# Two tables of x from the host, a scale from squares, and GpSimd for one third of the low halves

## What is computed

```
h = x @ W + b_W;  xi, xj = split(h)
xji = (xj[src] + (edge_attr @ W_e + b_We)) / (in_degree[dst] + 1e-6)
x  = layernorm(x + xi + segment_sum(xji, dst))
h2 = x @ W1;  deg counts the edges and one self loop per node
out = segment_sum(h2[src] * rsqrt(deg)[src] * rsqrt(deg)[dst], dst) + b1
y  = leaky_relu(batchnorm(out) * gamma + beta, 0.01)
result = layernorm(x + y)
```

## Time and profile before

| what | value |
|---|---|
| median of 3 runs | 936.38 us (935.14 to 938.89) |
| the profiled execution | 936.68 us, of which the span of the trace is 934.6 us |
| busy share of the span | PE 95%, DVE 72%, ACT 48%, POOL 37% |
| DMA | 244.77 MB, mean 262 GB/s |

### The profile page before, as it was taken

How to read it: one execution, slowest core, us unless ns; L and a number is a source line. 1 busy time by engine, 2 the same in 40 slices (tenths; PEclk the granted TensorE clock), 3 DMA queues, 4 the chain that set the end, 5 groups by cost and what they waited for, 6 DMA issues and landing times.

```text
span 934.6 us, 30500 instructions
## 1 busy us (share of the span) xinstructions
PE 883.9 (95%) x12210; PEld 791.2 (85%) x12210; DVE 676.6 (72%) x1249; ACT 450.3 (48%) x983; POOL 349.4 (37%) x401
## 2 busy tenths in 40 slices
PE   4867999999999999999999999999999999999995
PEld 4756888888988898989899999999988888888874
DVE  6999899999999998899888899888842111112255
ACT  3764666656666665556565556565542000000026
POOL 2236444455554444455334455434332011112200
PEclk8988999999999999999999999999999999999998
DMA  6428999998879788777878758678667897779654
GB/s 180 110 83 296 361 345 320 317 342 290 313 247 319 284 311 283 229 229 241 253 264 277 223 185 301 214 274 282 209 216 299 343 358 279 272 260 326 249 155 136
DMA packets 96762, 244.77 MB, mean 262 GB/s; under 512 B 39560, under 2 KB 64838, under 8 KB 90726
## 3 DMA queue, kind: packets, MB, share of 16 engines
q1 hardware_dynamic: 95014, 239.46, 73.7%
q0 software_dynamic: 1600, 3.28, 1.4%
HBM read 183.85 MB, written 58.85 MB: 260 GB/s over the span
## 4 chain that ended last, share of the span: by engine, by line
PE 85%; DVE 5%; issue 3%; ACT 3%; DMA 1%; SPq 1%; ACTq 0%; DVEq 0%
PE x_ps L876 26%; PE pair_ps L951 19%; PE pair_ps L858 13%; PE e_ps L895 10%; PE x_ps L884 9%; PE j_ps L933 2%; PE j_ps L981 2%; DVE lo_oh L616 1%; DVE key_oh L619 1%; PE pair_ps L960 1%; PE j_ps L934 1%; ACT counts L1065 1%; PE u_vps L1409 1%; DMA counts_kept<-counts 1%; DMA streams<-in_x 1%
## 5 line engine op out<-in xcount | busy, mean ns | idle before, releaser
L1065 ACT CAST counts<-pair_ps 128x784 bf16<-128x784 f32 x391 | 315.3, 817 | 251.5 <-PE pair_ps L858 244.1
L876 PE MATMUL x_ps<-counts,xsplit 128*128 128x256 bf16 (+1 forms) x2450 | 307.5, 271 | 0.0
L616 DVE TENSOR_TENSOR lo_oh<-counter,lo_t 128x2048 bf16<-128x2048 bf16 x196 | 252.3, 1287 | 53.9 <-PE pair_ps L858 52.5
L876 PEld LDWEIGHTS x_ps<-counts,xsplit 128*128 128x128 f16 x2450 | 222.1, 98 | 29.3 <-issue 7.1
L858 PE MATMUL pair_ps<-key_oh,lo_oh 128*128 128x100 bf16 x3128 | 207.8, 209 | 22.5 <-ACT counts L1065 15.4
L858 PEld LDWEIGHTS pair_ps<-key_oh,lo_oh 128*128 128x128 bf16 x3128 | 182.8, 98 | 36.9 <-issue 15.0
L619 DVE TENSOR_TENSOR key_oh<-counter,key_t 128x1600 bf16<-128x1600 bf16 x196 | 196.4, 1002 | 0.0
L895 PE MATMUL e_ps<-streams 128*32 128x128 f32 x3528 | 106.9, 274 | 0.1
L884 PE MATMUL x_ps<-counts,zown 128*128 128x256 bf16 (+1 forms) x840 | 105.9, 269 | 0.1
L951 PE MATMUL pair_ps<-streams,zown 128*128 128x256 bf16 x878 | 99.0, 273 | 0.0
L895 PEld LDWEIGHTS e_ps<-streams 128*32 128x32 f32 x3528 | 93.3, 110 | 4.8 <-issue 1.0
(11 more groups left out here) (181 smaller groups left out, 890.6 us busy)
## 6 DMA issues: line engine op xcount, KB each, us to landing
streams<-in_edge_attr SPq DMA_DIRECT2D x196, 576.0 KB, 9.1
counts_kept<-counts SPq DMA_DIRECT2D x10, 1600.0 KB, 9.1
streams<-counts_kept SPq DMA_DIRECT2D x6, 1600.0 KB, 6.5
counts<-counts_kept SPq DMA_DIRECT2D x4, 1600.0 KB, 7.1
counts_kept<-counts SPq DMA_DIRECT2D x2, 3136.0 KB, 12.7
streams<-counts_kept SPq DMA_DIRECT2D x2, 3136.0 KB, 14.8
edst<-in_dst SPq DMA_DIRECT2D x196, 4.5 KB
streams<-in_x SPq DMA_DIRECT2D x3, 1024.0 KB, 5.7
```

Source lines behind the costliest of these rows:

```text
L616: dv.tensor_tensor(lo_oh[:, ring, :, :, :].rearrange("p r w k t -> p (r w) k t"), counter[:, :, :].unsqueeze(1).to_broadcast([P, g, P, 2]) ...
L876: last = nc.tensor.matmul(x_ps[:, 0, 0:n], xsplit[:, q // 2, q % 2, :], by_hi[:, q // 2, :], start=(q == 0), stop=(q == 2 * HS - 1))
L1065: a.copy(out.rearrange("p h (g n) -> p h g n", g=2), pair_ps[at % 2][:, :, 0:4 * KW].rearrange("p g (n h) -> p h g n", h=HI)[:, 0:HS]).the ...
```

## The change

The kernel gets x in two more forms, both laid out by the host with no arithmetic: `x_rows` (a node's features in one partition, as in `xrows`) and `x_columns` (features on partitions). The columns are loaded into the memory of `zown`, and `own_product` reads them there; `turn_x` and `x_turned` are gone. The scale comes from the sum of all squares, not from the largest magnitude: PE multiplies each tile's upper bf16 halves by themselves (`sum_squares`), DVE takes the diagonal (`add_squares`), PE sums over partitions, DVE makes the power of two on all partitions (`scales`). The largest magnitudes per row are taken for the check alone, from the high halves, in blocks 16, 18 and 20. The high halves are at slots 7, 9 and 11, two of the low ones on DVE at slots 14 and 16, the third on POOL in two passes. SP loads both tables before the edges, waits for the low halves by chunk, and issues `keep_counts(0)` before the last of those chunks; in later blocks `keep_counts` stands one place earlier, and the load of row starts later. `count_row` and `start_of` move from slots 9 and 10 to 11 and 12.

```diff
 X_PIECES = ((0, 8), (8, 16), (16, NB))
-LARGEST_AT = (None, 2, 4)
-TOP_AT, SCALES_AT, SPREAD_AT = 5, 8, 12
-HIGH_AT, LOW_AT = (11, 13, 15), (16, 18, 20)
+NORM_AT, TOTAL_AT, SCALES_AT = 7, 5, 8
+HIGH_AT, LOW_AT = (7, 9, 11), (14, 16)
+ROWS_CHECKED_AT = (16, 18, 20)
 OWN = [(h, min(4, HS - h)) for h in range(0, HS, 4)]
-OWN_FIRST = 4
+SQUARED_FIRST = 4
+OWN_IN = {**{s: s + 1 for s in range(9)}, **{SL + 1 + k: 10 + k for k in range(3)}}
+SQUARED_IN = {1: (4, 5, 6, 7), 3: (8, 9, 10, 11, 12)}
...
-        own = zown[:, :].bitcast(F32).rearrange("p (h f) -> p h f", f=F)
+        columns = zown[:, :].bitcast(F32)
+        own = columns.rearrange("p (h f) -> p h f", f=F)
...
-        turn_ps = [x_ps[:, :, :].rearrange("p a (b n) -> p (a b) n", n=P), e_ps]
+        own_ps = [j_ps, e_ps]
+        squares_ps, norm_ps = x_ps[:, 0, 0:P], x_ps[:, 1, 0:1]
+        upper_halves = zown[:, :].bitcast(BF16).rearrange("p (h n q) -> p h n q", n=P, q=2)[:, :, :, 1]
...
-            sp.dma_start(wi, W0[:, 0:F]).then_inc(S["wi_in"], 16)
-            load_inputs(sp, {"x": xf}, x, S, range(1))
+            load_pieces(sp, columns, x_columns, S["columns_in"], range(1))
             for b in range(2, ROW_RING):
                 load_rows(sp, b)
+            sp.dma_start(wi, W0[:, 0:F]).then_inc(S["wi_in"], 16)
             load_weights(sp, {"wj": wj, "we": we, "bi": bi, "bj": bje, "be": be_t[:, :]}, W0, b0, We, be, S)
             sp.wait_ge(win_in[0], 32)
-            load_inputs(sp, {"x": xf}, x, S, range(1, len(X_PIECES)))
+            load_pieces(sp, columns, x_columns, S["columns_in"], range(1, len(X_PIECES)))
+            load_pieces(sp, xf, x_rows, S["x_in"], range(len(X_PIECES)))
 
             def start_values(b):
                 sp.wait_ge(S["starts_known"], b + 1)
...
+            def load_edges(b, g, starts):
+                reach(sp, S["e_summed"], edge_group(b - 1, g) + 1)
+                for c in range(EG):
+                    if b == 0 and g == 1:
+                        sp.wait_ge(S["x_low"], [(c + 1) * EJ * F <= 2 * z * F for _, z in X_PIECES].index(True) + 1)
+                        if c == EG - 1:
+                            keep_counts(0)
+                    sp.dma_start(ebuf[g][:, c, :, :].rearrange("p j f -> p (j f)"),
+                                 ea[bass.ds(starts[g * EG + c], EE), :].rearrange("(p j) f -> p (j f)", j=EJ))\
+                      .then_inc(e_in[g], 16)
 
...
+            load_rows(sp, ROW_RING)
             for b in range(NB + 2):
                 u = b - 2
-                if b + ROW_RING < LATE:
-                    load_rows(sp, b + ROW_RING)
-                if b + ROW_RING == LATE:
-                    load_late_rows(sp)
                 if b < NB:
                     starts = start_values(b)
                     load_destinations(b, starts)
+                    if 2 <= b <= NB - 2:
+                        keep_counts(b - 1)
                     keep_inverse(b)
-                if 1 <= b <= NB - 2:
...
+                if b + ROW_RING + 1 < LATE:
+                    load_rows(sp, b + ROW_RING + 1)
+                if b + ROW_RING + 1 == LATE:
+                    load_late_rows(sp)
...
+            def split_low(k):
+                at = piece_tiles(k)
+                pool.wait_ge(S["x_high"], k + 1)
+                step(g.tensor_scalar(xrows[:, at, :], xrows[:, at, :], xscale[:, 0:1], None, ALU.mult))
+                pool.wait_ge(S["x_low"], k)
+                g.tensor_tensor(xsplit[:, at, 1, :], xrows[:, at, :], xsplit[:, at, 0, :], ALU.subtract)\
+                 .then_inc(S["x_low"], 1)
...
+                if b == 0:
+                    split_low(2)
...
+            def add_squares():
+                dve.wait_ge(S["squares_summed"], 1)
+                step(dv.tensor_tensor(x1_mem[:, 0, :], squares_ps, ident[:, :], ALU.mult))
+                dv.tensor_reduce(out=norm[:, :], in_=x1_mem[:, 0, :], axis=AX.X, op=ALU.add).then_inc(S["norm_ready"], 1)
+
...
+            def scales():
+                dve.wait_ge(S["norm_out"], 1)
+                step(dv.tensor_copy(top[:, :], norm_ps))
+                dv.tensor_scalar(sound[:, 0:1], top[:, :], SQUARE_LEAST, None, ALU.is_ge)
+                dv.tensor_scalar(sound[:, 1:2], top[:, :], SQUARE_MOST, None, ALU.is_le)
+                step(dv.tensor_scalar(half_exp[:, :], top[:, :].bitcast(I32), 24, P - 1,
+                                      ALU.logical_shift_right, ALU.bitwise_and))
+                scale_i = xscale[:, :].bitcast(I32)
+                dv.tensor_scalar(scale_i[:, 0:1], half_exp[:, :], -float(ONE_EXP), float((190 + X_TOP) * ONE_EXP),
+                                 ALU.mult, ALU.add)
+                dv.tensor_scalar(scale_i[:, 1:2], half_exp[:, :], float(ONE_EXP), float((64 - X_TOP) * ONE_EXP),
+                                 ALU.mult, ALU.add).then_inc(S["scale_ready"], 1)
+                dve.wait_ge(S["scale_ready"], 1)
+
+            def row_largest(k):
...
+                step(dv.tensor_reduce(out=rowmax[:, at], in_=xsplit[:, at, 0, :], axis=AX.X,
+                                      op=ALU.max, apply_absolute_value=True))
...
+            for b in range(2, 4):
+                find_below(b)
+                pick_rows(b)
             ready_own_weights()
             dv.memset(total[:, :], 0.0)
             step(dv.tensor_copy(ebase[:, :], ebase_i[:, :]))
-            largest(0)
             make_keys(0)
-            for b in range(2, 4):
-                find_below(b)
-                pick_rows(b)
...
-                        if s in LARGEST_AT:
-                            largest(LARGEST_AT.index(s))
+                        if s == NORM_AT:
+                            add_squares()
                         if s == SCALES_AT:
                             scales()
-                        if s == SPREAD_AT:
-                            spread_scales()
                         if s == 3:
                             invert_degrees(0)
+                    if s == 7 and b in ROWS_CHECKED_AT:
+                        row_largest(ROWS_CHECKED_AT.index(b))
                     if SL * b + s in LOW_AT:
...
+                if b == 0:
+                    pe.wait_ge(S["own_added"], len(OWN))
...
+                first, last = ([end <= 2 * z for _, z in X_PIECES].index(True) for end in (h + 1, h + n))
+                for k in range(first, last + 1):
+                    pe.wait_ge(S["columns_in"][k], 16)
+
+            def sum_squares(m):
+                columns_here(m)
+                h, n = OWN[m]
+                for k in range(h, h + n):
+                    last = nc.tensor.matmul(squares_ps, upper_halves[:, k, :], upper_halves[:, k, :], start=(k == 0), stop=(k == HS - 1))
+                last.then_inc(S["columns_squared"], 1)
+                if m == len(OWN) - 1:
+                    pe.wait_ge(S["columns_squared"], len(OWN))
+                    pe.sem_inc(S["squares_summed"], 1)
 
             def own_product(m):
                 h, n = OWN[m]
+                columns_here(m)
                 pe.wait_ge(S["weights_ready"], 1)
-                pe.wait_ge(S["xT_out"], m + 1)
-                reach(pe, S["own_added"], m)
+                reach(pe, S["own_added"], m - 1)
                 for k in range(n):
-                    last = nc.tensor.matmul(j_ps[:, k, :], xT[m % 2][:, k, :], wi,
-                                            start=True, stop=True)
...
-            for b in range(2):
+            for b in range(ROW_RING):
                 find_rows(b)
-            for m in range(OWN_FIRST):
-                turn_x(m)
-                if m >= 1:
-                    own_product(m - 1)
+            for m in range(SQUARED_FIRST):
+                sum_squares(m)
             turn_keys(0)
-            for b in range(2, 4):
-                find_rows(b)
...
-                        if s == TOP_AT:
-                            pe.wait_ge(S["few_ready"], 1)
-                            pe.wait_ge(S["tabled"], 2)
-                            nc.tensor.transpose(few_ps[0:1, 0, 0:P], pmax[:, :], ident[:, :]).then_inc(S["few_out"], 1)
-                        if s == SCALES_AT + 1:
-                            pe.wait_ge(S["few_ready"], 2)
-                            nc.tensor.matmul(few_ps[:, 1, 0:4], ones[0:1, :], few[0:1, :].bitcast(F32),
-                                             start=True, stop=True).then_inc(S["few_out"], 1)
-                        if OWN_FIRST <= OWN_FIRST + s - 1 < len(OWN):
-                            own_product(OWN_FIRST + s - 1)
-                        if OWN_FIRST + s < len(OWN):
-                            turn_x(OWN_FIRST + s)
+                        for m in SQUARED_IN.get(s, ()):
+                            sum_squares(m)
+                        if s == TOTAL_AT:
+                            pe.wait_ge(S["norm_ready"], 1)
+                            nc.tensor.matmul(norm_ps, ones[:, :], norm[:, :], start=True, stop=True).then_inc(S["norm_out"], 1)
```

(47 more changed lines are left out.)

100 lines of the change are left out of this document (27 added, 73 removed).

## The result

The changed kernel takes 944.57 us, median of 3 runs (944.43 to 954.14), against 936.38: ratio 1.0112, 95% interval 1.0085 to 1.0139. The forecast of 926.0 us and its range to 934 are both missed. The profiled execution has a span of 942.8 us, where the kernel before had 934.6.

What follows compares the result with a forecast made beforehand. DVE was taken to bound the first blocks and a full PE everything from block 4 on. The terms -5.2 - 10.3 + 2.9 + 6.2 - 4.3 = -10.7 us gave 926.0 us, with an 8-in-10 range of 919.5 to 934.

Steps and rivals of the forecast that it cites:

- Start: Ahead of block 0: with the copies gone, the first one-hots start at 14.3 us instead of 19.54, -5.2 us.
- Work off DVE and onto DVE: Blocks 0 and 1: reductions, scale steps, copy and third low half leave DVE, -10.3 us; diagonal, scale steps and waits come, +2.9.
- GpSimd's two passes: Third low half on POOL: DVE stands still during the subtraction (4.2 us) and scaling (1.5 to 2.0), taken as +6.2 us.
- rival A: DVE loses the whole duration of POOL's passes, 10.2 instead of 6.2 us, giving 930.0 us; 20%.
- two-input slope: DVE's loss beside POOL elementwise steps with two inputs: 1.8 to 1.9 ns per column.
- one-input slope: DVE's loss beside a POOL step with one input: some 0.7 to 0.9 ns per column, from a 128-column step.
- forecast's upper bound: DVE's loss to POOL's passes at whole duration of undisturbed steps: 5.9 us with one input, 4.3 with two, together 10.2.
- Blocks 2 and 3: Block 0's counts are stored earlier, so ACT's wait goes and both blocks last 24.5 us: -4.3 us.
- The three later reductions: Blocks 16, 18 and 20: DVE's free time and the ring cover them, so they cost nothing; without that cover 7 us.
- Carry the shift to the end unchanged: From the start of block 4 on: the shift gained by then stays to the end, because the chain is full.
- All of the change lies before 80 us, except three reductions: Whole kernel: after 80 us only the reductions in blocks 16, 18 and 20 differ.
- D: Slower: POOL's passes take 53 us, end at about 96 us and hold up DVE, PE and SP, 957 us; 8%.

Runs made afterwards that it cites:

- e3: Changed kernel with SyncE's old order from block 2 on, count_row and start_of back at slots 9 and 10, and no three later reductions: 929.9 us.
- e1: Changed kernel with SyncE's old order from block 2 on (row loads at the block's head, keep_counts behind keep_inverse): 929.2 us, 0.9903 of before.
- e5: Changed kernel with only keep_inverse ahead of keep_counts again from block 2 on, row loads left where the change puts them: 929.2 us, 0.9909 of before.
- e9: Changed kernel with keep_inverse ahead of keep_counts again, plus an extra store in 8-byte packets behind the counts to rows nobody reads: 941.1 us.
- e13: Changed kernel with 64 more PE instructions, four semaphore increments in each slot of block 1: 949.9 us, 1.0142 of before.
- e15: Changed kernel with 192 more PE instructions, six semaphore increments in each slot of blocks 0 and 1: 957.9 us, 1.0206 of before.
- e7: Changed kernel with SyncE's old order from block 2 on and the third low half on DVE in one instruction: 923.6 us, 0.9853 of before.
- e12: Kernel before, with only the store of the inverse degrees moved behind the second group of edge loads from block 2 on: 940.9 us, 1.0050 of before.
- e8: Kernel before, with only SyncE's new order from block 2 on (moved row loads, keep_counts ahead of keep_inverse): 962.1 us, 1.0242 of before.
- e6: Changed kernel with only the row loads back at the head of a block, keep_counts left ahead of keep_inverse: 946.7 us, 1.0087 of before.

## Why the prediction was wrong

Point by point, by its own steps:

- *Start*, -5.2 us: first one-hots at 13.58 us instead of 19.54, so -6.0. Right.
- *Work off DVE and onto DVE*, -10.3 and +2.9: blocks 0 and 1 take 59.9 us. With GpSimd's cost at what it measured (below), 58.1 - 10.3 + 2.9 + 9.4 = 60.1. Right together, not measured apart.
- *GpSimd's two passes*, +6.2: mis-sized. Timelines of POOL and DVE, kernel after:

```profile
41.93 5.88 POOL L516 TENSOR_SCALAR streams<-streams,xscale 128x2176 f32<-128x2176 f32 x1 [3.37 <-ACT xsplit L1119]
47.90 4.92 POOL L518 TENSOR_TENSOR xsplit<-streams,xsplit 128x2176 f16<-128x2176 f32 x1
...
42.13 6.52 DVE L618 TENSOR_TENSOR lo_oh<-counter,lo_t 128x2048 bf16<-128x2048 bf16 x1
48.58 5.08 DVE L621 TENSOR_TENSOR key_oh<-counter,key_t 128x1600 bf16<-128x1600 bf16 x1
```

  DVE loses 6.52 - 1.22 = 5.3 us and 5.08 - 0.99 = 4.1 us, together 9.4. So rival A ("the whole duration is lost", 10.2 us, 20%) is what happened. The two-input slope held (1.9 ns a column). The one-input slope, taken from a step of 128 columns, was off by three: 2.4 ns a column instead of 0.7 to 0.9. The rows that the slope came from can be read otherwise: POOL's two steps took 3.13 us there and 1.19 where DVE had little to do, so it was probably POOL that waited, and such a row can't tell what DVE loses. (The 2.6 ns in the forecast's upper bound stands in no row; 2.4 was measured.) Here DVE and GpSimd exclude each other for the whole of the one-input step too, as the Trainium skill's rule (SBUF — State Buffer, Who interferes with whom) would have it if taken word for word.
- *Blocks 2 and 3*, -4.3 us: both last 24.5 us. Right.
- *The three later reductions*, nothing: e3, without them, is no faster than e1 (929.9 and 929.2 us). Right.
- *"Carry the shift to the end unchanged"*: this step failed, and it decided the sign. It rests on another sentence, "All of the change lies before 80 us, except three reductions", and that is wrong: SyncE's new order of stores and row loads holds in every block from 2 on and has no term in the sum. That order puts 128 packets of 8 bytes behind each store of counts, the queues move 158 to 231 GB/s behind most of them instead of about 400, PE's instruction packets come late and PE stops: 15.4 us (e1, e5), of which an extra store of tiny packets behind the counts brings back 12.0 (e9). That late packets are what stops PE is shown by the count of its instructions at the stalls, above all in e13 to e15. With the old order the rest of the forecast stands: e1's 929.2 us is 926.0 and the 3.2 us by which GpSimd was underpriced. That this agrees to a tenth is luck: the interval of e1's ratio reaches from 923.6 to 930.9 us.

None of the rivals had this mechanism. D, the slower one, did not happen: POOL's passes ended at 52.8 us. Stalls of this kind are also there without the swap (1.24 us before, 1.99 us in e7), only fewer and shorter. Open is why the tiny packets slow the queues only behind the counts, why e12 is slower than before, what makes the 3.5 us between e9 and the changed kernel, and why e8 costs more than e6.

## What to carry to other kernels

A full PE is not a safe bound if the queues are full beside it: before a lead is carried forward, price every reordered DMA to the end of the loop, small stores above all, and keep packets of a few bytes from behind a large store. Gaps of PE named "issue", at lines that have nothing in common, ask for a look at the instruction queue, and it can be tested by adding idle instructions and counting where in the stream the gaps begin. A GpSimd pass over a long tile beside DVE steps with two inputs should be priced at its whole duration on DVE, whatever short steps suggest.

## What was not expected of the hardware

- 128 packets of 8 bytes behind a store of 1.6 to 3.2 MB halve what the queues move in the next 5 us (158 to 231 GB/s instead of 361 to 417), with the DMA engines as busy as before; the same packets 0.5 us ahead of it don't.
- PE's instruction stream is itself DMA traffic of 1.64 MB, and its packets come up to some 10 us late when the queues are full. In 76 of 77 stalls PE stopped at the same count, 193 past a multiple of 256. With 64, 128 and 192 instructions more that do nothing the medians were 5.3, 9.6 and 13.4 us higher; only the last is clear of the intervals. So when the queues are full a difference of 1% between two kernels can be no more than the place of its packets.
- The granted clock fell to 0.50 for over 3 us behind stalls of 2.73 us at 202 us and 2.80 us at 287 us (block 10's mean clock is 0.95), and stayed at 1.00 around the ones of 1.35, 2.11 and 1.58 us in blocks 8, 16 and 20. The length alone doesn't decide: in e7 it fell to 0.50 for over 3 us behind the stall of 1.99 us at 217 us.
